# Two loads exchanged at the start, and two weight splits moved behind a bias and a sum, in a conditioned low-rank linear kernel

## The chip, the cores and the metric

The kernel runs on one core of one Trainium2 chip. The metric is device time in microseconds; the kernel before took 918.89 us, the median of three runs (918.77 to 919.0).

## The reference

For each of 128 batch entries (64 channels by 1024 columns) the input is first mixed over channels with one of 16 weight blocks of 64 by 64, chosen by an integer condition. The result y goes through a linear layer W with bias b (1024 to 1024) and, beside it, through eight low-rank maps of rank 16. The low-rank part m is scaled by a clamped ratio of norms, and x is added back:

```
y = einsum('bct,bcd->bdt', x, weights[condition])
z = einsum('bsd,od->bso', y, W) + b
u = einsum('bsd,edr->ebsr', y, A)
m = einsum('ebsr,ero,e->bso', u, B, p_scores)
gamma = minimum(0.5 * norm(z) / (norm(m) + 1e-6), 1.0)
out = x + z + gamma * m
```

All inputs and the output are float32.

## The kernel before

Two batch entries make a tile of 128 rows; there are 64 tiles in 32 pairs. The two tiles of a pair are called 0 and 1 (slots r = 0 and 1).

**Numbers in two parts.** TensorE multiplies in the type fp32r. Each operand is split in a high part, a cast on ACT (ScalarE), and a low part, the difference, on VectorE. A product is then three passes per chunk of 128 rows: high by high, high by low, low by high.

**Products of a pair.** W is cut in four quadrants W11, W12, W21, W22. Pair 0 uses them directly (`plain...`). From pair 1 on a scheme with seven products instead of eight runs, P1 to P7, on sums of y (S1 to S4) and of quadrants (T1 to T4): `product_y` and `product_s` at L984. P1 is y of tile 0 by W11, P2 by W21, P4 is y of tile 1 by T4, P6 is S2 by T2, P5 is S1 by T1, P7 is S3 by T3, P3 is S4 by W22. `down` and `up` are the low-rank part (L1049, L1053, L1068), and `mix` (L970) multiplies the next tiles by their mixer blocks.

**PSUM.** The bank b_ps is used by P1, P2, P6 and P7 in turn. P1's result leaves it in `bias_p1` (L796), and only then may P2 start. P2's leaves in `make_z11` (L775), after which P6 may start. m_ps is emptied by the sum of m1 (`add_m1`, L757), and then tile 0's `up` may start. The next pair's mix of tile 1 may overwrite a half of mix_ps once `split_y` (L691) has made the low part of the tile 0 that lay there.

**What sets the order.** Each engine has one written list of instructions and takes them in that order; semaphores join the lists. Nothing is planned at run time. SP and ACT also issue loads, each on a DMA queue of its own (q1 for SP, q10 for ACT in the profile).

**The start.** SP issues the load of the conditions, then x's tile 1, then waits for the conditions, issues the mixer blocks of half 0 of both tiles (`first_mixer`) and after them the chunks of W12 and W11 in turn (L286), W21, W22 and the rest. ACT issues x's tile 0 and, once the conditions are there, its mixer block for tile 0 (L533), W11's first chunk (L534) and its mixer block for tile 1 (L535). Then its computing starts with `split_w(W11, (0,))` (L438), followed by the copies of tile 0's y (L454) and of W12's first chunk. TensorE runs idle matmuls (L1090), mixes tile 0, makes two passes of W11's first chunk (L1003, L1005), mixes tile 1 (from x's tile 1 and the mixer blocks of tile 1), and goes on with `plain_first_half`.

**The stretch of pair 1.** The T matrices are made and split once, between 23 and 59 us. VectorE's order for pair 1 is: the low parts of T4 (two halves, L682), the low part of y's tile 1 and the sums S3 and S2 (L691, L699, L707), T2's first half, P1's bias, tile 1's residual of pair 0 (L852), gamma, m1's sum, T2's second half, S2's low part and so on. ACT casts the high parts of T4 and T2 ahead of the squares of z1 and m1 (L507, L516), with y's tile 1 between T2's halves.

Of the kernel before, what the change touches and what calls it, by code (L numbers as in the profile page):

```python
# [5 lines left out]
def conditioned_clamped_low_rank_linear_kernel(  # L6
# [29 lines left out]
    B, C, D = x.shape  # L36
    E = cond_w.shape[1]
    _, X, R = a.shape
    P = 128
    PER = P // C  # L40
# [9 lines left out]
    W11, W21, W22, T1, T2, T3, T4 = range(7)  # L50
# [7 lines left out]
    x_tiles = x.rearrange("(n q) c t -> n (q c) t", q=PER)  # L58
    out_tiles = out.rearrange("(n q) c t -> n (q c) t", q=PER)

    w_blocks = {n: w[h * H:(h + 1) * H, o * H:(o + 1) * H].rearrange("(k p) o -> k p o", p=P)
                for n, h, o in ((W11, 0, 0), (W12, 0, 1), (W21, 1, 0), (W22, 1, 1))}

    ctx = ExitStack()
    with ctx:  # L65
        def sb(name, shape, dt):
            return ctx.enter_context(nc.sbuf_tensor(name, shape, dt))
# [4 lines left out]
        def sem(name):  # L72
            return ctx.enter_context(nc.semaphore(name))
# [18 lines left out]
        x_in = sb("x_in", [P, 4, D], fp32)  # L92
# [22 lines left out]
        def stat(n, r):  # L115
            return stats[:, 6 + 2 * n + r:7 + 2 * n + r]
# [8 lines left out]
        raw11 = w_hi_raw[:, T1, :, :]  # L125
# [17 lines left out]
        x_loaded = [sem(f"x_loaded{s}") for s in range(4)]  # L143
# [3 lines left out]
        w_loaded = {n: [sem(f"w{name}_{k}_loaded") for k in range(HC)]  # L147
                    for n, name in ((W11, "11"), (W12, "12"), (W21, "21"), (W22, "22"))}
# [93 lines left out]
        def t_count(n, g):  # L242
            return 2 * T_ORDER.index(n) + g + 1


        def chunks(operand, g):
            return operand[:, 2 * g:2 * g + 2, :]
# [10 lines left out]
        def first_condition(engine, t, q):  # L258
            n = t * PER + q
            return engine.value_load(cond_ids[0:1, n:n + 1], min_val=0, max_val=E - 1)  # L260

        def first_mixer(t, q):
            return mixer[q * C:(q + 1) * C, t, q * C:(q + 1) * C]

        def cond_block(e):
            return cond_w[:, bass.ds(e, 1), :].rearrange("c e d -> c (e d)")

        def s_raw(n):
            return {S1: s14[:, 0, :, :], S4: s14[:, 1, :, :], S2: s23[:, 0, :, :], S3: s23[:, 1, :, :]}[n]
# [4 lines left out]
        def _(sp):  # L274
# [11 lines left out]
                    sp.dma_start(raw[n][:, k, :], w_blocks[n][k]).then_inc(w_loaded[n][k], 16)  # L286

            sp.dma_start(cond_ids[:, :], condition.rearrange("(o n) -> o n", o=1)).then_inc(ids_loaded, 16)
            sp.dma_start(x_in[:, 1, :], x_tiles[1]).then_inc(x_loaded[1], 16)
            sp.wait_ge(mixer_zeroed, 1)  # L290
            sp.wait_ge(ids_loaded, 16)
            sp.dma_start(first_mixer(0, 0), cond_block(first_condition(sp, 0, 0))).then_inc(mixer_loaded[0], 16)
# [140 lines left out]
        def _(act):  # L433
# [6 lines left out]
            def split_t(n, g):  # L440

                act.wait_ge({T1: t1_made, T2: t2_made, T3: t3_made, T4: t4_made}[n], g + 1)
                if n == T4:
                    act.wait_ge(plain_done, 4)
                elif n == T1:
                    act.wait_ge(t3_made, g + 1)
                elif n == T3:
                    act.wait_ge(t_lo_ready, t_count(T4, g))
                nc.scalar.copy(chunks(w_hi[:, n, :, :], g), chunks(raw_t[n], g)).then_inc(t_hi_ready, 1)

            def split_y(t, r, h, source=mixed):

                act.wait_ge(mix_done, halves(t, h))
                nc.scalar.copy(y_part(y_hi, r, h), source(h)).then_inc(y_hi_ready, 1)  # L454
# [7 lines left out]
            def split_s(p, n, first=False):  # L462

                act.wait_ge({S1: s1_made, S2: s2_made, S3: s3_made, S4: s4_made}[n], p)
                if not first:
                    act.wait_ge(p_done[{S1: 5, S2: 6, S3: 7, S4: 3}[n]], p - 1)
                nc.scalar.copy(s_hi[:, n, :, :], s_raw(n)).then_inc(s_hi_ready, 1)  # L467
# [30 lines left out]
            def square_z1(p, opening):  # L498

                act.wait_ge(z21_ready, p + 1)  # L500
                act.wait_ge(z22_ready, p + 1)
                if opening:
                    act.wait_ge(z12_squared, 1)
                else:
                    act.wait_ge(m_squared[0], p)
                    act.wait_ge(norm_z_ready[1], p)
                nc.scalar.activation(squares[:, :], z1[:, :], ACT.Square,  # L507
                                     accum_out=stat(Z_SQ, 1)).then_inc(z1_squared, 1)

            def square_m1(p, opening):  # L510

                act.wait_ge(m_done[1], p + 1)
                act.wait_ge(z1_squared, p + 1)
                if not opening:
                    act.wait_ge(norm_m_ready[1], p)
                nc.scalar.activation(squares[:, :], m_ps[:, :], ACT.Square,  # L516
                                     accum_out=stat(M_SQ, 1)).then_inc(m_squared[1], 1)
# [13 lines left out]
            act.wait_ge(mixer_zeroed, 1)  # L531
            act.wait_ge(ids_loaded, 16)
            act.dma_start(first_mixer(0, 1), cond_block(first_condition(act, 0, 1))).then_inc(mixer_loaded[0], 16)  # L533
            act.dma_start(raw11[:, 0, :], w_blocks[W11][0]).then_inc(w_loaded[W11][0], 16)  # L534
            act.dma_start(first_mixer(1, 1), cond_block(first_condition(act, 1, 1))).then_inc(mixer_loaded[1], 16)  # L535
            split_w(W11, (0,))
            split_y(0, 0, 0)
# [27 lines left out]
            split_t(T2, 0)  # L565
            for h in range(2):
                split_y(3, 1, h)
            split_t(T2, 1)
            square_z1(0, True)
            square_m1(0, True)  # L570
            split_s(1, S2, True)
            split_t(T1, 0)
            split_t(T1, 1)
            split_s(1, S3, True)
# [64 lines left out]
        def _(dve):  # L639
# [34 lines left out]
            def split_t(n, g):  # L674

                dve.wait_ge(t_hi_ready, t_count(n, g))
                if n == T2:
                    dve.wait_ge(t4_made, g + 1)
                    dve.wait_ge(t3_made, g + 1)
                elif n == T1:  # L680
                    dve.wait_ge(t2_made, g + 1)
                nc.vector.tensor_tensor(chunks(w_lo[:, n, :, :], g), chunks(raw_t[n], g),  # L682
                                        chunks(w_hi[:, n, :, :], g).bitcast(fp32), ALU.subtract
                                        ).then_inc(t_lo_ready, 1)

            def split_y(p, r, h, opening=False, source=mixed):

                dve.wait_ge(y_hi_ready, halves(2 * p + r, h))
                if r == 0 and not opening:
                    dve.wait_ge(y_copied, 2 * p + h - 1)  # L690
                nc.vector.tensor_tensor(y_part(y_lo, r, h), source(h), y_part(y_hi, r, h).bitcast(fp32),  # L691
                                        ALU.subtract).then_inc(y_lo_ready, 1)
# [33 lines left out]
            def make_half_over_m(p, r):  # L726

                dve.wait_ge(norm_m_ready[r], p + 1)
                nc.vector.tensor_scalar(stat(TWICE_M, r), stat(NORM_M, r), EPS, 1.0 / CLAMP, ALU.add,  # L729
                                        ALU.mult).then_inc(twice_m_ready[r], 1)  # L730
                dve.wait_ge(twice_m_ready[r], p + 1)
                nc.vector.reciprocal(stat(HALF_OVER_M, r), stat(TWICE_M, r)).then_inc(over_m_ready[r], 1)  # L732

            def limit_gamma(p, r):

                dve.wait_ge(norm_z_ready[r], p + 1)
                dve.wait_ge(over_m_ready[r], p + 1)  # L737
                nc.vector.tensor_scalar(stat(GAMMA, r), stat(NORM_Z, r), stat(HALF_OVER_M, r), 1.0, ALU.mult,  # L738
                                        ALU.min).then_inc(gamma_ready[r], 1)

            def make_gamma(p, r):

                make_half_over_m(p, r)
                limit_gamma(p, r)
# [8 lines left out]
            def add_m1(p):  # L753

                dve.wait_ge(gamma_ready[1], p + 1)
                dve.wait_ge(residual1_ready, p + 1)
                nc.vector.scalar_tensor_tensor(out=z1[:, :], in0=m_ps[:, :], scalar=stat(GAMMA, 1), in1=z1[:, :],  # L757
                                               op0=ALU.mult, op1=ALU.add).then_inc(out1_ready, 1)
# [34 lines left out]
            def bias_p1(p, par):  # L793

                dve.wait_ge(p_done[1], p)
                nc.vector.tensor_tensor(z0[:, par, up_], b_ps[:, :], bias[:, 1, :], ALU.add).then_inc(p1_biased, 1)  # L796
# [44 lines left out]
            dve.wait_ge(z12_squared, 1)  # L841
            nc.vector.tensor_tensor(z0[:, 0, :], z0[:, 0, :], x_in[:, 0, :], ALU.add).then_inc(residual0_ready, 2)
            split_t(T4, 0)
            split_t(T4, 1)
            split_y(1, 1, 0)
            make_s3(1, True)
            split_y(1, 1, 1)
            make_s2(1, True)
            split_t(T2, 0)
            bias_p1(1, 1)  # L850
            dve.wait_ge(z1_squared, 1)
            nc.vector.tensor_tensor(z1[:, :], z1[:, :], x_in[:, 1, :], ALU.add).then_inc(residual1_ready, 1)  # L852
            make_gamma(0, 1)
            add_m1(0)
            split_t(T2, 1)
            split_s(1, S2)
            dve.wait_ge(s2_made, 1)
# [375 lines left out]
```

## Time and profile before

| | us |
|---|---|
| median of three runs | 918.89 |
| profiled execution | 919.13 |
| its span | 917.3 |
| TensorE matmul busy | 908.7 (99%) |
| VectorE busy | 589.2 (64%) |
| ACT busy | 368.5 (40%) |
| GpSimd busy | 319.9 (35%) |

The busy times are shares of one profiled execution. The granted clock of TensorE is given as a share of full speed; over the whole span it was 0.999. TensorE's share says that the steady part is bound by its matmuls; the two places that the change touches lie in the first 63 us, where ACT and VectorE have more to do than later.

### The profile page before, as it was taken

How to read it: one execution, taken by the hardware profiler on the slowest of the kernel's cores; microseconds unless marked ns; L12 is line 12 of the kernel's file. 1: busy time of each engine (PE TensorE's matmuls, PEld its weight loads, DVE VectorE, ACT ScalarE, POOL GpSimd, SP SyncE). 2: the span in 40 equal slices, each digit the busy share in tenths (PEclk: the TensorE clock that was granted, in tenths of full speed). 3: DMA queues.
4: the chain of work that ended last, by engine and by line, in shares of the span. 5: the costliest groups of instructions: out<-in, count | busy, mean ns of one | idle time of the engine just before them, and what ended most of it. 6: DMA issues, size and time to landing. Idle time of an engine off the chain costs nothing. (4 is left out here: it accounts for less than half of the span.)

```text
span 917.3 us, 14774 instructions
## 1 busy us (share of the span) xinstructions
PE 908.7 (99%) x4642; PEld 773.7 (84%) x4642; DVE 589.2 (64%) x938; ACT 368.5 (40%) x732; POOL 319.9 (35%) x316
## 2 busy tenths in 40 slices
PE   8999999999999999999999999999999999999997
PEld 6888888888888888888888888888888888888886
DVE  6996757566665557665566656666655756566665
ACT  6653433434334334434343343334333443434333
POOL 0123443224433234432344332443323443224432
PEclk9999999999999999999999999999999999999999
DMA  8212222122221222211222212222112222122211
GB/s 295 81 71 95 95 72 83 37 91 94 71 94 46 71 94 81 85 68 49 94 94 71 94 40 78 94 71 94 49 68 94 94 71 79 40 93 94 73 47 69
DMA packets 32745, 75.17 MB, mean 82 GB/s; under 512 B 12761, under 2 KB 13786, under 8 KB 32730
## 3 DMA queue, kind: packets, MB, share of 16 engines
q1 hardware_dynamic: 32138, 73.91, 22.9%
q10 hardware_dynamic: 592, 1.08, 0.4%
q8 instruction: 7, 0.11, 0.1%
q14 instruction: 8, 0.07, 0.0%
HBM read 41.42 MB, written 33.55 MB: 82 GB/s over the span
## 5 line engine op out<-in xcount | busy, mean ns | idle before, releaser
L454 ACT CAST y<-mix_ps 128x512 fp32r<-128x512 f32 x126 | 74.3, 591 | 298.2 <-PE mix_ps L970 298.2
L386 POOL TENSOR_TENSOR stats<-stats 128x1 f32<-128x1 f32 x31 | 17.2, 556 | 451.2 <-ACT squares L507 451.2
L984 PE MATMUL b_ps<-w_hi,y 128*128 128x512 f32 x510 | 167.8, 389 | 0.0
L712 DVE TENSOR_TENSOR s_lo<-s,s_hi 128x512 fp32r<-128x512 f32 x124 | 134.6, 1105 | 4.2
L970 PEld LDWEIGHTS mix_ps<-mixer,x_in 128*128 128x128 f32 x1008 | 122.0, 191 | 6.8 <-issue 2.0
L970 PE MATMUL mix_ps<-mixer,x_in 128*128 128x128 f32 x1008 | 122.7, 275 | 1.2 <-DMA mixer<-in_L_cond_weights_dram 1.2
L467 ACT CAST s_hi<-s 128x512 fp32r<-128x512 f32 x124 | 76.7, 618 | 114.5 <-POOL s L360 93.4
L372 POOL TENSOR_TENSOR z<-z,x_in 128x512 f32<-128x512 f32 x61 | 79.1, 1296 | 113.8 <-ACT squares L488 107.3
L984 PEld LDWEIGHTS b_ps<-w_hi,y 128*128 128x128 f32 x510 | 95.7, 188 | 20.2 <-DVE z L796 0.3
L691 DVE TENSOR_TENSOR y<-mix_ps,y 128x512 fp32r<-128x512 f32 x126 | 86.4, 687 | 38.2 <-ACT s L460 38.2
L984 PE MATMUL b_ps<-w_lo,y 128*128 128x512 f32 x255 | 99.2, 389 | 0.0
L984 PE MATMUL c_ps<-w_hi,s_hi 128*128 128x512 f32 (+1 forms) x248 | 98.7, 398 | 0.0
L984 PE MATMUL c_ps<-w_lo,s_hi 128*128 128x512 f32 (+1 forms) x248 | 96.2, 388 | 0.0
L984 PE MATMUL c_ps<-w_hi,s_lo 128*128 128x512 f32 (+1 forms) x248 | 96.2, 388 | 0.0
L984 PE MATMUL b_ps<-w_lo,s_hi 128*128 128x512 f32 x244 | 94.9, 389 | 0.0
L984 PE MATMUL b_ps<-w_hi,s_hi 128*128 128x512 f32 x244 | 94.9, 389 | 0.0
L984 PE MATMUL b_ps<-w_hi,s_lo 128*128 128x512 f32 x244 | 94.9, 389 | 0.0
L984 PE MATMUL a_ps<-w_hi,y 128*128 128x512 f32 x264 | 87.1, 389 | 0.0
L770 DVE TENSOR_TENSOR z<-b_ps,z 128x512 f32<-128x512 f32 x30 | 20.8, 692 | 101.5 <-PE b_ps L984 101.5
L366 POOL TENSOR_TENSOR z<-z,x_in 128x1024 f32<-128x1024 f32 x30 | 72.1, 2404 | 0.0
L1049 PE MATMUL u_ps<-y,a_hi 128*128 128x512 f32 x256 | 69.3, 392 | 0.0
L791 DVE TENSOR_TENSOR z<-a_ps,bias 128x512 f32<-128x512 f32 x31 | 21.4, 691 | 57.7 <-PE a_ps L984 57.7
(156 smaller groups left out, 1584.9 us busy)
## 6 DMA issues: line engine op xcount, KB each, us to landing
x_in<-in_x_dram SPq DMA_DIRECT2D x63, 512.0 KB, 3.6
out_dram<-z SPq DMA_DIRECT2D x62, 512.0 KB, 2.8
w_lo_raw<-in_L_ffn_W_dram SPq DMA_DIRECT2D x8, 256.0 KB, 6.6
mixer<-in_L_cond_weights_dram SPq DMA_DIRECT2D x126, 16.0 KB, 2.1
w_hi_raw<-in_L_ffn_W_dram SPq DMA_DIRECT2D x7, 256.0 KB, 6.7
out_dram<-z SPq DMA_DIRECT2D x3, 256.0 KB, 2.0
x_in<-in_x_dram ACTq DMA_DIRECT2D x1, 512.0 KB, 3.3
a_lo_raw<-in_L_ffn_A_dram SPq DMA_DIRECT2D x1, 512.0 KB, 8.2
```

The lines of the kernel that those rows point to most:

```text
L366: nc.gpsimd.tensor_tensor(z1[:, :], z1[:, :], x_in[:, slot, :], ALU.add).then_inc(residual1_ready, 1)
L372: nc.gpsimd.tensor_tensor(z0[:, par, cols], z0[:, par, cols], x_in[:, 2 * par, cols], ALU.add).then_inc(residual0_ready, 1)
L386: nc.gpsimd.tensor_tensor(stat(NORM_Z, 1), stat(Z_SQ, 1), half, ALU.pow).then_inc(norm_z_ready[1], 1)
L454: nc.scalar.copy(y_part(y_hi, r, h), source(h)).then_inc(y_hi_ready, 1)
L467: nc.scalar.copy(s_hi[:, n, :, :], s_raw(n)).then_inc(s_hi_ready, 1)
L691: nc.vector.tensor_tensor(y_part(y_lo, r, h), source(h), y_part(y_hi, r, h).bitcast(fp32), ALU.subtract).then_inc(y_lo_ready, 1)
L712: nc.vector.tensor_tensor(s_lo[:, n, :, :], s_raw(n), s_hi[:, n, :, :].bitcast(fp32), ALU.subtract).then_inc(s_lo_ready, 1)
L770: nc.vector.tensor_tensor(z1[:, up_], bank[:, :], z0[:, par, up_], ALU.add).then_inc(u3_ready, 1)
L791: nc.vector.tensor_tensor(z1[:, lo], a_ps[:, :], bias[:, 2, :], ALU.add).then_inc(p4_biased, 1)
L970: made = nc.tensor.matmul(source(h)[:, k, :], x_in[:, slot, (h * HC + k) * P:(h * HC + k + 1) * P], mixer[:, r, :], start=True, stop=True)
L984: summed = nc.tensor.matmul(bank, left[:, k, :], right[:, n, k, c], start=(start and k == 0 and i == 0), stop=(stop and k == HC - 1 and i ...
L1049: return nc.tensor.matmul(u_ps[:, :], a_hi[:, k, :], y[:, k, :, :], start=(k == 0), stop=(k == KC - 1))
```

## The change

SP now issues W11's first chunk where it issued x's tile 1, and ACT issues x's tile 1 where it issued W11's first chunk. On ACT, T2's second half is cast after the squares of z1 and m1 and S2's high part. On VectorE the low parts of T4's second half and of T2's first half move: T4's behind P1's bias and tile 1's residual, T2's behind m1's sum. The number of instructions and of bytes is unchanged.

```diff
             sp.dma_start(cond_ids[:, :], condition.rearrange("(o n) -> o n", o=1)).then_inc(ids_loaded, 16)
-            sp.dma_start(x_in[:, 1, :], x_tiles[1]).then_inc(x_loaded[1], 16)
+            load_w(W11, (0,))
             sp.wait_ge(mixer_zeroed, 1)
             sp.wait_ge(ids_loaded, 16)
@@ on ACT
             act.dma_start(first_mixer(0, 1), cond_block(first_condition(act, 0, 1))).then_inc(mixer_loaded[0], 16)
-            act.dma_start(raw11[:, 0, :], w_blocks[W11][0]).then_inc(w_loaded[W11][0], 16)
+            act.dma_start(x_in[:, 1, :], x_tiles[1]).then_inc(x_loaded[1], 16)
             act.dma_start(first_mixer(1, 1), cond_block(first_condition(act, 1, 1))).then_inc(mixer_loaded[1], 16)
...
             for h in range(2):
                 split_y(3, 1, h)
-            split_t(T2, 1)
             square_z1(0, True)
             square_m1(0, True)
             split_s(1, S2, True)
+            split_t(T2, 1)
@@ on VectorE
             split_t(T4, 0)
-            split_t(T4, 1)
             split_y(1, 1, 0)
             make_s3(1, True)
             split_y(1, 1, 1)
             make_s2(1, True)
-            split_t(T2, 0)
             bias_p1(1, 1)
             dve.wait_ge(z1_squared, 1)
             nc.vector.tensor_tensor(z1[:, :], z1[:, :], x_in[:, 1, :], ALU.add).then_inc(residual1_ready, 1)
+            split_t(T4, 1)
             make_gamma(0, 1)
             add_m1(0)
+            split_t(T2, 0)
             split_t(T2, 1)
```

## Rows read from the trace of the kernel before

**Rows 1.** Busy, 11-62 us: PE, PEld, DVE, ACT, POOL, granted clock, DMA share, GB/s.
```profile
11.00:62.00 51.00, 51.00 (x256) 42.70 (x255) 49.98 (x70) 33.49 (x55) 5.46 (x5) 1.00 0.40 142
```

**Rows 2.** Order of time at the start: start us, us, instruction, idle before it.
```profile
3.99 0.59 ACTq L534 DMA_DIRECT2D w_hi_raw<-in_L_ffn_W_dram  x1
...
5.32 0.48 ACTq L535 DMA_DIRECT2D mixer<-in_L_cond_weights_dram  x1
...
5.84 2.02 PE L970 MATMUL mix_ps<-mixer,x_in 128*128 128x128 f32 x16 [1.25 <-DMA mixer<-in_L_cond_weights_dram]
...
7.00 0.62 ACT L438 CAST w_hi<-w_hi_raw 128x512 fp32r<-128x512 f32 x1 [4.34 <-DMA w_hi_raw<-in_L_ffn_W_dram]
...
8.73 1.95 PE L970 MATMUL m_ps<-mixer,x_in 128*128 128x128 f32 x16
8.95 0.62 ACT L438 CAST w_hi<-w_lo_raw 128x512 fp32r<-128x512 f32 x1 [0.36 <-DMA w_lo_raw<-in_L_ffn_W_dram]
...
10.43 0.69 DVE L691 TENSOR_TENSOR y<-m_ps,y 128x512 fp32r<-128x512 f32 x1
...
10.74 0.39 PE L984 MATMUL c_ps<-w_hi,y 128*128 128x512 f32 x1
...
11.43 0.39 PE L984 MATMUL a_ps<-w_hi,y 128*128 128x512 f32 x1
```

**Rows 3.** DMA issues at 1 to 2 and 5.2 to 5.8 us: KB, us to landing.
```profile
x_in<-in_x_dram SPq DMA_DIRECT2D x1, 512.0 KB, 4.2
...
mixer<-in_L_cond_weights_dram ACTq DMA_DIRECT2D x1, 16.0 KB, 3.2
```

**Rows 4.** The page's part 6, all mixer loads of SP: KB, median us to landing.
```profile
mixer<-in_L_cond_weights_dram SPq DMA_DIRECT2D x126, 16.0 KB, 2.1
```

**Rows 5.** Half microseconds from 6.0 on, columns as in rows 1.
```profile
6.00:6.50 0.50, 0.50 (x6) 0.50 (x6) 0.00 (x0) 0.00 (x0) 0.00 (x0) 1.00 0.40 129
6.50:7.00 0.50, 0.50 (x7) 0.50 (x6) 0.00 (x0) 0.00 (x1) 0.00 (x0) 1.00 0.38 99
7.00:7.50 0.50, 0.50 (x7) 0.50 (x6) 0.00 (x0) 0.50 (x1) 0.00 (x0) 1.00 0.86 305
```

**Rows 6.** Order of time on VectorE (DVE) from 35 to 69 us.
```profile
35.16 0.69 DVE L691 TENSOR_TENSOR y<-mix_ps,y 128x512 fp32r<-128x512 f32 x1 [0.29 <-ACT s L460]
...
38.63 2.35 DVE L682 TENSOR_TENSOR w_lo<-w_hi_raw,w_hi 128x1024 fp32r<-128x1024 f32 x2
...
42.70 0.68 DVE L707 TENSOR_TENSOR s<-mix_ps,s 128x512 f32<-128x512 f32 x1
...
44.43 0.68 DVE L796 TENSOR_TENSOR z<-b_ps,bias 128x512 f32<-128x512 f32 x1
...
46.86 1.28 DVE L757 SCALAR_TENSOR_TENSOR z<-m_ps,stats,z 128x1024 f32<-128x1024 f32 x1
...
51.53 0.69 DVE L775 TENSOR_TENSOR z<-b_ps,bias 128x512 f32<-128x512 f32 x1
...
61.71 1.28 DVE L691 TENSOR_TENSOR y<-mix_ps,y 128x512 fp32r<-128x512 f32 x2
...
68.73 0.69 DVE L780 TENSOR_TENSOR z<-c_ps,z 128x512 f32<-128x512 f32 x1 [1.23 <-PE c_ps L984]
```

**Rows 7.** Who waited for whom, 38 to 63 us: total us, times, longest.
```profile
PEld m_ps L1068 <- DVE z L757: 0.4, 1, 0.4
...
PEld b_ps L984 <- DVE z L796: 0.3, 1, 0.3
```

**Rows 8.** Order of time on TensorE (PE) from 42 to 63 us.
```profile
42.08 0.39 PE L984 MATMUL b_ps<-w_hi,y 128*128 128x512 f32 x1
...
52.46 0.39 PE L984 MATMUL b_ps<-w_hi,s_hi 128*128 128x512 f32 x1
...
62.21 0.39 PE L984 MATMUL b_ps<-w_hi,s_lo 128*128 128x512 f32 x1
...
62.54 0.68 PE L970 MATMUL mix_ps<-mixer,x_in 128*128 128x128 f32 x4
```

## The prediction, made before the changed kernel was run

> **What bounds the kernel now.** I read the busy times by stretch first. From 11 to 62 us TensorE is busy for all of it and VectorE for 49.98 us of 51.00 [rows 1]; the reader should see that two engines are full at once there, and that a TensorE on 100% says nothing of short waits, since ends of matmuls are modelled. So I went on to the order of time at the start, for the two loads that change places [rows 2], then to the times from issue to landing [rows 3, 4] and to the DMA's free share [rows 5], then to VectorE's order of time in the stretch where the splits move [rows 6], and last to TensorE's waits and starts there [rows 7, 8]. The spacing of 512-column matmuls is 0.23 us (three of them from 10.74 to 11.43 [rows 2]).
>
> Two things come out. The start is a chain: the mixer block lets the first mix begin at 5.84, ACT then holds tile 0's copy back because it casts W11's first chunk only at 7.00, and the mix of tile 1 starts at 8.73 [rows 2]. Later, from 35.16 on, VectorE has no wait ahead of an instruction until 68.73, where it idles 1.23 us for TensorE [rows 6]. In that run its y split at 61.71 ends at 62.39, and TensorE's next mix begins at 62.54 [rows 6, 8], where the product ahead would have let it go at 62.44 (its last matmul starts at 62.21, one spacing earlier). So at 62.54 TensorE is released by VectorE, by 0.10 us, and whatever TensorE won before that point is lost in that wait unless VectorE's own chain gets shorter. From there on VectorE has slack, so what the kernel's end moves by is what the start at 62.54 moves by.
>
> **The loads.** Let g be the time by which TensorE's work after the start moves ahead. W11's first chunk is now issued at SP's second place and lands well before the 7.00 at which ACT now starts on it [rows 2]. ACT (0.62 us) and VectorE split it while TensorE waits for the mixer block. That block's issue doesn't move, nor do I move the 5.84: bounds 0.2 us earlier (fewer bytes ahead) and 0.2 later; I take 0. ACT copies tile 0's first half as soon as the first half of the mix ends, near 6.95 and not at 7.52 (behind 7.00 and 0.62), so the two first passes of W11 follow the mix at 7.86 (5.84 and 2.02) and are over by about 8.1, where before they were followed at 8.73.
>
> Then comes tile 1's mix, which wants two things. x's tile 1 is issued at 3.99 on ACT's queue in place of a load half its size: x's tile 1 took 4.2 us to landing when it stood behind tile 0's load [rows 3], so it is there at 8.2 at the latest that I expect. ACT's mixer block for tile 1 is issued behind it at 5.32 and took 3.2, landing at 8.5 [rows 2, 3]; at the median of 2.1 [rows 4] it would be there at 7.4. So the mix starts at 8.6 if nothing changes for that block (g is 0.1), at 8.2 if it comes early. The next term is W12's first chunk: ACT starts on it at 8.95, having waited for the DMA [rows 2]. Between 6.0 and 7.0 the DMA engines were at 0.40 and 0.38 of their time [rows 5], 0.61 us free in all. The half us after it moved 305 GB/s at a share of 0.86 [rows 5], 355 at full share, by which the added 256 KB want 0.74 us of all engines. So I count W12 as 0.1 us late; the bounds are 0 and the whole 0.7. VectorE's parts of that chunk and of y, 0.60 each, then end near 10.9 and not at 11.11 (10.43 and 0.68), which lets the product on y of tile 1 start up to 0.3 before its 11.43 [rows 2]. g is therefore at most 0.3, and at least -0.4 (0.7 of lateness less the 0.3). I take 0.2, between the 0.1 of an unchanged mixer block and the 0.3.
>
> The Trainium skill's DMA: Bandwidth & Descriptors, section Queues, rings and completion order, says that each DMA engine goes round-robin over the queues that have work and serves one packet of descriptors of one queue before it takes the next. In the trace the mixer block issued at 5.32 took 3.2 us against a median of 2.1 [rows 3, 4], as if on some engines W12 of the other queue had gone ahead of it. By the rule that block would now stand right behind x's tile 1 and before W12, g would be 0.3, and the sum 0.1 us lower: that is rival (e).
>
> **Does g reach 62.54?** VectorE's run begins at 35.16 with a wait of 0.29 us for ACT's copy of the mix [rows 6], which TensorE releases; no other wait stands in it. So VectorE's chain moves by g with TensorE, both ways.
>
> **The moved splits.** On VectorE a 1024-column split takes 1.13 us of the engine and a 512-column operation 0.60: 38.63 to 42.70 is two and three of them, 42.70 to 44.43 one and one [rows 6]. Before, p1's bias starts at 44.43. Now T4's second part and T2's first part are no longer ahead of it, and the queue reaches it at 38.63 + 1.13 + 4 x 0.60 = 42.16. But it waits for P1, whose last matmul starts at 42.08 and ends 0.39 later [rows 8]; with 0.03 for the release, an estimate, VectorE starts at 42.50. So 0.34 us of idle time goes into a run that had none. It hits the work behind it: residual of tile 1 (1.13), T4's part (1.13), gamma (0.70: 44.43 + 0.60 + 1.13 is 46.16, and m1's sum starts at 46.86 [rows 6]) and m1's sum, which now starts at 46.06 and not at 46.86, then both parts of T2. From there on the set of finished work is that of before, 0.34 later: z11 at 51.87 instead of 51.53, the y split of 61.71 at 62.05.
>
> On TensorE two waits go: for p1's bias (the loader idle 0.3) and for m1's sum (0.4) [rows 7]. Less the 0.04 between loads that is usual, that is at most 0.6 us; by starts of matmuls I make it 0.46. It comes at P6, which started at 52.46 [rows 8], by then about 0.55 earlier, and finds z11 unready: 51.87 and 0.69 are 52.56, and so it starts at 52.62. The stall removed is late again as a stall on z11. Even without it TensorE would stand at the mix of 62.54 until y's split, now 0.34 later. On ACT, T2's second cast stands behind the squares of z1 and m1 now; TensorE wants T2 at P6, 8 us later, and the squares come sooner for it. The transfers that residual 1 and m1's sum release start 0.8 to 2 us earlier, in a stretch where the DMA has room (share 0.40 over the 51 us [rows 1]). I count these at 0; bounds 0.1 either way.
>
> **Sum.** Start -0.2 (+0.4 to -0.3), VectorE's new wait +0.34 (0 to 0.35), the removed TensorE waits 0 (down to -0.10, the wait at 62.54 that would go if VectorE were earlier). That is +0.14. The profiled execution took 919.13 (span 917.3), so 919.27 for one like it; the median of the three runs, 918.89, is 0.24 below it, which makes 919.03.
>
> **Rivals.** What a measurement here can tell from no change is about 0.2%, 1.84 us.
> (a) *The reordering pays.* TensorE's removed waits stay won because VectorE isn't what releases it at 62.54 and P1's end is met without idle time: -0.46 - 0.2, 918.2. For it: the waits of rows 7 are real. Against: a run of 26 us without a wait on VectorE. Half of it, no idle time of 0.34 but the wait at 62.54 kept, gives 918.7.
> (b) *The loads are late.* Tile 1's 512 KB and the mixer block behind it collide with W12's first chunk on the DMA engines; it decides from the point where that chunk lands over 0.25 us after the 8.95 of before. ACT casts it ahead of y, so TensorE stands at the product on y. At 0.7 late g is -0.4, and with the 0.34 that is 919.6. For it: ACT already waits for that load. Against: the free 0.6 us between 6.0 and 7.0 [rows 5].
> (c) *The clock falls.* If TensorE stands longer before tile 1's mix and the granted clock goes to the lower of its levels (1.2 instead of 2.4 GHz), the 4 us of matmuls from 8.73 take twice as long: 923. Against: the granted clock is 1.00, and the wait before 5.84, over a microsecond long, did not lower it.
> (d) *Nothing moves*: VectorE finds P1 done, the start is bound by W12 alone, g is 0 to 0.1, and nothing is added: 918.8 to 918.9.
> (e) *The mixer block gains.* Tile 1's block lands about 1 us earlier, at its median of 2.1 from issue, since W12 is no longer served ahead of parts of it; then g is its full 0.3 and the time 919.13 - 0.3 + 0.34 - 0.24 = 918.93. For it: the 3.2 us of rows 3 with the DMA at 0.4 of its time. Against: it still stands behind a load, now of twice the bytes. It is what the Trainium skill's rule on queues gives.
>
> **How the numbers follow.** Forecast, the wait on P1 taking back the start's gain (918.9 to 919.3): 0.25; (d) 0.1; (e) 0.17, the same wait on P1 with the larger g. (a) in whole or half: 0.2. (b): 0.25. (c) 0.03. For the range I take from half of (a) up through (b), with 0.1 us of scatter of a median: 918.4 to 919.7. By the bound of 0.2% only (c) and something unforeseen leave "same": same 0.94, slower 0.04, faster 0.02.
>
> **What would show it.** In the changed kernel's order of time: ACT's cast of W11 before 5.84 and its y cast at about 7.0; the mix of tile 1 between 8.2 and 8.7; on VectorE a wait of 0.3 us on b_ps ahead of p1's bias near 42.3; no wait on VectorE at the TensorE starts of P2 and of up(0), but one on z11 at P6; the mix of 62.54 at 62.68, still right behind the y split. Wrong would be: W12's cast after 9.2, no idle time before p1's bias, or a mix near 62.5 that comes straight behind the product.

## The result, and the profile after

The changed kernel took 920.16 us (median of 22 runs, 919.75 to 921.53) against 918.87 (22 runs, 918.62 to 920.83): a ratio of 1.0015, 95% interval 1.001 to 1.0021. It is 1.29 us slower, where 919.03 was forecast and 919.7 was the upper end. The profiled execution took 920.47 with a span of 918.6 and a granted clock of 0.999.

The start of the changed kernel in order of time (start us, us, instruction, idle before it); these lines answer to [rows 2]:

```profile
3.55 0.59 ACTq L534 DMA_DIRECT2D x_in<-in_x_dram  x1
...
4.87 0.48 ACTq L535 DMA_DIRECT2D mixer<-in_L_cond_weights_dram  x1
...
5.40 0.62 ACT L438 CAST w_hi<-w_hi_raw 128x512 fp32r<-128x512 f32 x1 [2.75 <-DMA w_hi_raw<-in_L_ffn_W_dram]
5.80 2.16 PE L970 MATMUL mix_ps<-mixer,x_in 128*128 128x128 f32 x16 [0.38 <-DMA mixer<-in_L_cond_weights_dram]
...
8.07 0.40 PE L1005 MATMUL b_ps<-w_lo,y 128*128 128x512 f32 x1
...
9.21 2.02 PE L970 MATMUL m_ps<-mixer,x_in 128*128 128x128 f32 x16 [0.74 <-DMA mixer<-in_L_cond_weights_dram]
9.56 0.62 ACT L438 CAST w_hi<-w_lo_raw 128x512 fp32r<-128x512 f32 x1 [0.98 <-DMA w_lo_raw<-in_L_ffn_W_dram]
...
11.31 0.40 PE L984 MATMUL c_ps<-w_hi,y 128*128 128x512 f32 x1
```

W11's cast is early and the passes on it end before 8.5, as meant. In this execution what they won is spent in a wait for tile 1's mixer block, and tile 1's mix starts at 9.21 instead of 8.73. The repeat of the changed kernel (e1 below) was as slow by another way: its mixes are early, and TensorE waits for the low part of W12's first chunk, which ACT casts at 9.59. Its lines:

```profile
8.46 2.02 PE L970 MATMUL m_ps<-mixer,x_in 128*128 128x128 f32 x16 [0.65 <-DMA mixer<-in_L_cond_weights_dram]
...
9.59 0.62 ACT L438 CAST w_hi<-w_lo_raw 128x512 fp32r<-128x512 f32 x1 [1.67 <-DMA w_lo_raw<-in_L_ffn_W_dram]
...
11.08 0.47 PE L984 MATMUL c_ps<-w_hi,y 128*128 128x512 f32 x1 [0.36 <-DVE w_lo L644]
```

So two loads are late, and which of them TensorE feels differs from one execution to the next; W12's cast is late in both. The DMA issues of the changed kernel from 4.8 to 5 us, and those from 3 to 4.2 (KB, us to landing), say when the block and x's tile 1 were there; they answer to [rows 3]:

```profile
mixer<-in_L_cond_weights_dram ACTq DMA_DIRECT2D x1, 16.0 KB, 4.2
...
x_in<-in_x_dram ACTq DMA_DIRECT2D x1, 512.0 KB, 3.6
```

x's tile 1 was there at 7.15, two microseconds before it was used. The block behind it took 4.2 us instead of 3.2; in the repeat it took 3.4, where the kernel before took 3.4 in its own repeat (e13), so the 4.2 is no fixed cost. In the half microseconds from 6.5 on (columns as in [rows 1], to be read against [rows 5]), the DMA engines moved little in this execution:

```profile
6.50:7.00 0.50, 0.50 (x7) 0.50 (x6) 0.24 (x1) 0.00 (x0) 0.00 (x0) 1.00 0.44 91
7.00:7.50 0.50, 0.50 (x7) 0.50 (x6) 0.00 (x0) 0.40 (x1) 0.00 (x0) 1.00 0.41 37
7.50:8.00 0.50, 0.50 (x6) 0.50 (x5) 0.28 (x1) 0.19 (x2) 0.00 (x0) 1.00 0.14 31
```

In the repeat the share in these slices is 0.50, 0.65 and 0.90, and W12's first chunk landed 4.7 us behind its issue in both. The low share is therefore not the mark of the loss.

VectorE in the changed kernel, which answers to [rows 6]:

```profile
42.14 0.68 DVE L707 TENSOR_TENSOR s<-mix_ps,s 128x512 f32<-128x512 f32 x1
43.08 0.69 DVE L796 TENSOR_TENSOR z<-b_ps,bias 128x512 f32<-128x512 f32 x1 [0.27 <-PE b_ps L984]
...
46.14 0.16 DVE L732 RECIPROCAL stats<-stats 128x1 f32<-128x1 f32 x1
46.85 0.21 DVE L738 TENSOR_SCALAR stats<-stats 128x1 f32<-128x1 f32 x1 [0.54 <-DVE stats L732]
47.10 1.28 DVE L757 SCALAR_TENSOR_TENSOR z<-m_ps,stats,z 128x1024 f32<-128x1024 f32 x1
...
63.08 1.28 DVE L691 TENSOR_TENSOR y<-mix_ps,y 128x512 fp32r<-128x512 f32 x2
```

Two waits stand in the run that had none. From S2's making to P1's bias it is 0.94 us and not 0.60: the forecast 0.34. The second wasn't forecast: 0.54 us idle ahead of gamma's last step (L738), though nothing that it waits for is late. Before the change the same step came 0.27 us after the start of the reciprocal ahead of it, now 0.71, so it adds 0.43 or 0.44. The two lines before the change:

```profile
46.34 0.16 DVE L732 RECIPROCAL stats<-stats 128x1 f32<-128x1 f32 x1
46.61 0.21 DVE L738 TENSOR_SCALAR stats<-stats 128x1 f32<-128x1 f32 x1
```

On TensorE, to be read against [rows 8]:

```profile
53.73 0.47 PE L984 MATMUL b_ps<-w_hi,s_hi 128*128 128x512 f32 x1 [0.88 <-DVE z L775]
...
63.91 1.35 PE L970 MATMUL mix_ps<-mixer,x_in 128*128 128x128 f32 x10
```

P6 stands 0.88 us for z11, and the mix of 62.54 comes at 63.91, right behind the y split that ends at 63.76. TensorE's wait for P1's bias is gone; the one for m1's sum, which was forecast to go, is still 0.3 us instead of 0.4, since m1's sum stands behind gamma. Nothing of what was won is left at 63.91.

### The profile page after: what moved, and what is told of

The parts are those of the page before. It is cut to its first block and busy times, and to the rows that moved or that the text cites. A ratio compares the mean times of both kernels' runs of the same rounds, so it can differ in the third digit from the quotient of the medians.

```text
span 918.6 us, 14774 instructions
## 1 busy us (share of the span) xinstructions
PE 909.6 (99%) x4642; PEld 773.8 (84%) x4642; DVE 589.3 (64%) x938; ACT 368.3 (40%) x732; POOL 319.0 (35%) x316
```

## The experiments

Two starts of mixes divide the time of every run. A is the mix of tile 0 of pair 1 (31.91 before), up to which only the loads matter. B is the mix of 62.54. What follows B is the profiled time less B; it is nearly constant (856.55 to 856.66) in all but e5, e10 and e11. The first column is the median less that of the kernel before on the same chip (22 runs of the changed kernel, 8 of e8, 11 of every other; 15 to 33 of before). The other columns are from one profiled execution each.

| run | median, less before | A | B | B - A | profiled time - B |
|---|---|---|---|---|---|
| before | | 31.91 | 62.54 | 30.63 | 856.59 |
| e13 before again | -0.08 | 31.83 | 62.46 | 30.63 | 856.57 |
| changed | +1.29 | 32.49 | 63.91 | 31.42 | 856.56 |
| e1 changed again | +1.31 | 32.37 | 63.83 | 31.45 | 856.56 |
| e2 loads only | +0.55 | 31.87 | 62.51 | 30.63 | 856.66 |
| e14 loads again | +0.54 | 32.14 | 62.78 | 30.63 | 856.59 |
| e3 splits only | +0.77 | 31.69 | 63.14 | 31.45 | 856.58 |
| e4 T4 before the bias | +0.46 | 31.47 | 62.52 | 31.06 | 856.55 |
| e5 waits added | +0.57 | 31.69 | 62.68 | 30.99 | 856.76 |
| e6 T2 before gamma | +0.33 | 31.95 | 62.94 | 30.99 | 856.56 |
| e7 block first | +0.91 | 32.83 | 63.47 | 30.63 | 856.56 |
| e8 both early | +2.50 | 32.89 | 63.52 | 30.63 | 856.56 |
| e9 x in halves | +0.31 | 31.77 | 62.39 | 30.62 | 856.56 |
| e10 residual on GpSimd | +0.61 | 32.29 | 63.35 | 31.06 | 856.72 |
| e11 e4 with waits | +0.38 | 32.15 | 62.77 | 30.63 | 856.78 |
| e12 half of x | +0.29 | 31.55 | 62.17 | 30.63 | 856.62 |
| e15 half of x again | +0.03 | 32.04 | 62.67 | 30.63 | 856.58 |

How to read it: B - A takes three values over 30.63, and each returns to within 0.03 wherever its cause is there. A scatters by 0.8 us (31.47 to 32.29) over the eight profiles with the loads of before, so a single profile says little of the start, and medians are used for it. An estimate of A in the median run is the median less the last two columns: 31.6 to 31.7 with the loads of before (but 31.8 in e11), 32.1 to 32.2 with the exchange. What decides A lies in the first 11 us: from the first product on c_ps (10.74 before, 11.31 in the changed kernel) to A it is 21.17 to 21.29 us in all 17 profiles. The runs' ratios have 95% intervals of 0.0009 either way (0.8 us), which includes most of these differences; it is B - A, together with the medians of 11, that carries the verdicts.

**The change again, and its two parts.** e1 is the changed kernel, e2 the first two hunks of the diff alone (SP's and ACT's loads), e3 all the others alone.

> The changed kernel once more, as a control. Its profile had tile 1's mix at 9.22 us (8.73 before), the first product on c_ps at 11.31 (10.74), 0.27 us of idle time ahead of P1's bias and 0.54 us ahead of gamma's last step, and the mix of 62.54 at 63.91. Theory: all of these come from the order of instructions and repeat, so about 1.3 us over before. Rival: the late start and the wait in gamma are scatter of one execution; then the mix of pair 1 comes at 62.9 to 63.9 in different runs and the median gain over before is smaller than in the profile.

> Only the exchange of W11's first chunk and x's tile 1; splits as before. Theory (the start's loss reaches the end): tile 1's mix near 9.2, c_ps near 11.3, the mix of 62.54 at 63.1, and 0.58 us over before (919.45 where before is 918.87). Rival (the prediction's g): the exchange gains 0.2 us when alone, 918.7. Rival 2: VectorE's slack takes the loss in and the time is that of before.

> Only the moved splits on ACT and VectorE; loads as before. Theory: 0.34 us idle ahead of P1's bias and 0.44 more than usual ahead of gamma's last step, TensorE stands on z11 at P6, the mix of 62.54 at 63.3; 0.78 us over before (919.65). Rival: the wait in gamma hangs on the moment at which loads or other engines work, and is not there: only 0.34 over before (919.2).

Ratios 1.0013 (1.0004 to 1.0022), 1.0007 (0.9998 to 1.0016), 1.0008 (0.9999 to 1.0018). The parts add up: 0.55 and 0.77 are 1.32, against 1.31. The loads act on A alone, the splits on B - A alone, by 0.82, with the wait in gamma in it. VectorE's slack takes in nothing. Not all that was expected repeated: tile 1's mix starts at 8.46 in e1 and at 8.60 in e2, and not near 9.2, and e2's B is 62.51 and not 63.1. The profile of e2 is of a fast execution (919.17, median 919.39), and its 0.55 rests on the median; e14 repeats it with 0.54.

**P1's wait alone taken away.** e4 is e3 with one line moved:

```diff
             make_s2(1, True)
+            split_t(T4, 1)
             bias_p1(1, 1)
...
-            split_t(T4, 1)
             make_gamma(0, 1)
```

> As the run with only the splits moved, but T4's second part stands behind S2 and ahead of P1's bias, where VectorE waited for P1. Theory: no idle time ahead of the bias, so 0.34 less than the run with only the splits moved; with the wait in gamma kept (its place in VectorE's list is the same) 0.44 over before (919.3). Rival: that wait hangs on time and goes too; then VectorE's chain is that of before, and the time is that of before or 0.1 less (918.8).

Measured: +0.46, ratio 1.0006 (0.9997 to 1.0015); B - A falls by 0.39 to 31.06, and no idle time is left ahead of the bias. The wait in gamma stayed, as the profile of e4 shows, and is the whole of what is left (0.43):

```profile
45.47 0.21 DVE L738 TENSOR_SCALAR stats<-stats 128x1 f32<-128x1 f32 x1 [0.54 <-DVE stats L732]
```

**What the wait in gamma hangs on.** e5 is e3 with waits that are fulfilled long before; e6 is e3 with T2's first part moved; e11 has the edits of e4 and e5.

```diff
             split_t(T4, 0)
+            dve.wait_ge(idle_set, 1)
+            dve.wait_ge(mixer_zeroed, 1)
+            dve.wait_ge(w_hi_ready, 1)
+            dve.wait_ge(a_hi_ready, 1)
             split_y(1, 1, 0)
```

```diff
             split_t(T4, 1)
+            split_t(T2, 0)
             make_gamma(0, 1)
             add_m1(0)
-            split_t(T2, 0)
             split_t(T2, 1)
```

> As the run with only the splits moved (its profile: 0.54 us idle ahead of gamma's last step, 0.11 before the change), with four waits that are long fulfilled put into VectorE's list behind T4's first part, where VectorE is busy: gamma's instructions stand two places further down VectorE's list, as before the change, and nothing else moves. Theory (the 0.43 hangs on the place of an instruction in VectorE's list, as code loading would): 0.11 again, and 0.34 over before (919.2) instead of 0.78. Rival (it hangs on what stands ahead of gamma, T4's second part, or on what other engines do at that time): 0.54 stays, and the time with it.

> As the run with only the splits moved, but T2's first part ahead of gamma and m1's sum instead of behind them. Theory (place in the list): gamma's last step stands where it stood before the change, so the 0.43 goes and only the 0.34 us of idle time ahead of P1's bias stay: 919.2. TensorE then waits for m1's sum at 48.2 and not only for z11. Rival (what matters is T4's part before gamma or the changed order of the squares on ACT): 0.54 stays idle, 919.6.

> The run with T4's second part ahead of P1's bias and the four fulfilled waits put behind T4's first part. Theory: neither the idle time ahead of P1's bias nor the 0.43 in gamma is there, VectorE's chain is as long as before the change, and so the mix comes 30.6 us after that of tile 0 of pair 1, as before; at the end the two places further down cost the 0.2 us that the run with the waits had in its last step. 919.05; without these 0.2, 918.85. Rival: the reordering costs by something else that these two waits only accompany; 919.3.

e5, then e6, in the order of time on VectorE:

```profile
45.34 0.16 DVE L732 RECIPROCAL stats<-stats 128x1 f32<-128x1 f32 x1
45.61 0.21 DVE L738 TENSOR_SCALAR stats<-stats 128x1 f32<-128x1 f32 x1
```

```profile
46.75 0.17 DVE L732 RECIPROCAL stats<-stats 128x1 f32<-128x1 f32 x1
47.02 0.21 DVE L738 TENSOR_SCALAR stats<-stats 128x1 f32<-128x1 f32 x1
```

In both the wait is gone, and B - A is 30.99, that is 0.36 for P1's wait alone. e5 changes no work and keeps T4's part ahead of gamma, so neither that nor what other engines do at the time makes the wait: the place in the list does. The packed traces say which place. They hold a record of each instruction of VectorE, waits that stand by themselves among them; the four waits of e5 come out as two records more than in e3. Gamma's last step is the 64th record of VectorE in all five profiles with 0.54 us ahead of it (changed, e1, e3, e4, e10), and the 66th in the twelve with 0.11. A second such place is the 192nd record. In the kernel before it is gamma's last step of a later pair; in e11, where that step is the 194th, the wait is gone, and in e10 (described below), where it is the 190th, the wait stands ahead of the sum behind it, which is now the 192nd. Before, e11, e10:

```profile
110.71 0.21 DVE L738 TENSOR_SCALAR stats<-stats 128x1 f32<-128x1 f32 x1 [0.47 <-DVE stats L732]
```

```profile
110.58 0.21 DVE L738 TENSOR_SCALAR stats<-stats 128x1 f32<-128x1 f32 x1
```

```profile
111.86 1.28 DVE L752 SCALAR_TENSOR_TENSOR z<-m_ps,stats,z 128x1024 f32<-128x1024 f32 x1 [0.49 <-DVE stats L740]
```

In e11 both waits of the changed kernel are gone and B - A is that of before. e5 and e11 cost more than their B - A says (+0.57 and +0.38); 0.2 of it is behind B, and the chain of waits at the end shows where. e5's, and behind it that of the kernel before (start us, us, what):

```profile
913.47 0.23 issue
913.69 0.75 DVE z L966
```

```profile
913.36 0.03 issue
913.38 0.75 DVE z L962
```

The same two places further down that take the wait out of gamma of pair 0 put one of 0.23 instead of 0.03 ahead of the last sum. The remaining 0.2 of e11 lies in A (32.15 in its profile), though its loads are those of before; that is open. e11's time is therefore 0.2 over the 919.05 that was expected, and it is B - A that says that the two waits are all that the moved splits cost.

**Less work on VectorE.** e10 is the kernel before, with its first residual on GpSimd:

```diff
@@ VectorE
-            dve.wait_ge(z11_squared, 1)
-            dve.wait_ge(z12_squared, 1)
-            nc.vector.tensor_tensor(z0[:, 0, :], z0[:, 0, :], x_in[:, 0, :], ALU.add).then_inc(residual0_ready, 2)
@@ GpSimd
+                        residual0(0, 0, 0)
+                        residual0(0, 0, 1)
                         norm_z1(0)
```

> The kernel before with one edit: the residual of pair 0's tile 0 (1.13 us of VectorE at 37.5) is done by GpSimd in two halves. Theory (VectorE's chain sets the mix of 62.54): the chain is 1.13 us shorter, TensorE's waits at 45.2, 48.2 and 62.5 all go, and the mix follows its product at once: 0.56 us less, 918.3. By the theory of the place in the list gamma's instructions now stand two places up, as in the changed kernel, and its last step is preceded by 0.54 us idle although no split was moved; the shorter chain hides it. Rival: GpSimd's adds slow VectorE down by as much, or the chain is bound elsewhere; 918.9.

Measured: +0.61, ratio 1.0007 (0.9998 to 1.0016), the opposite sign; the rival had it, but for the wait in gamma, which isn't hidden. In order of time, e10 around its residual:

```profile
36.12 1.28 POOL L372 TENSOR_TENSOR z<-z,x_in 128x512 f32<-128x512 f32 x1 [6.21 <-ACT squares L497]
36.15 2.34 DVE L673 TENSOR_TENSOR w_hi_raw<-w_hi_raw,w_lo_raw 128x1024 f32<-128x1024 f32 x1
...
47.42 0.21 DVE L740 TENSOR_SCALAR stats<-stats 128x1 f32<-128x1 f32 x1 [0.54 <-DVE stats L734]
```

The subtraction that makes T4's second half (L673) took 2.34 us instead of 1.22 beside GpSimd's add of 1.28: the 1.13 us taken off VectorE came back in the same place. So e10 does not show what a shorter chain on VectorE would give. Then comes the wait in gamma, of 0.54 as forecast, in a kernel in which no split was moved; two records were taken out ahead of it. B - A is 31.06, as in e4, the other run with that wait alone. e10 has 0.14 more behind B; that was not followed up.

**The loads.** e7 is e2 with ACT's last two issues exchanged; e8 is e2 with x's tile 1 on SP:

```diff
@@ e7, ACT
-            act.dma_start(x_in[:, 1, :], x_tiles[1]).then_inc(x_loaded[1], 16)
             act.dma_start(first_mixer(1, 1), cond_block(first_condition(act, 1, 1))).then_inc(mixer_loaded[1], 16)
+            act.dma_start(x_in[:, 1, :], x_tiles[1]).then_inc(x_loaded[1], 16)
@@ e8, SP (and ACT's load of x's tile 1 taken out)
             load_w(W11, (0,))
+            sp.dma_start(x_in[:, 1, :], x_tiles[1]).then_inc(x_loaded[1], 16)
```

> The exchanged loads alone, but ACT issues tile 1's mixer block ahead of x's tile 1. Theory 1 (the loss comes from the block standing behind 512 KB): the block lands by 7.2, tile 1's mix starts as soon as x's tile 1 is there, near 8.0, and the loss of 0.55 us of the exchange goes: 918.8 to 918.9. Theory 2 (W12's first chunk sets it, landing at 8.9 to 9.6 behind x's tile 1, against 8.6 to 8.9 before): tile 1's mix is early but the product on c_ps stays near 11, and the time is 919.2 to 919.5.

> The loads alone, but x's tile 1 on SP's queue right behind W11's first chunk, both ahead of the mixer blocks; ACT issues only x's tile 0 and its two blocks. Theory 1 and 2 both: nothing stands between the blocks and W12, which land by 7.5 and 8.7; the first mix is 0.3 to 0.6 us late, as the blocks of tile 0 stand behind 256 KB more, the mix of tile 1 starts at about 8.5. 918.8. If the bytes ahead of the blocks cost their whole 0.6 us, 919.2.

e7: +0.91, ratio 1.0008 (0.9999 to 1.0017); e8: 1.0027 (1.0017 to 1.0038). Both theories of e7 were too kind: the block was early, but x's tile 1 landed so late that TensorE waited for it, and W12's first chunk was cast at 10.09. e7's order of time:

```profile
9.05 2.05 PE L970 MATMUL m_ps<-mixer,x_in 128*128 128x128 f32 x16 [0.62 <-DMA x_in<-in_x_dram]
10.09 0.62 ACT L438 CAST w_hi<-w_lo_raw 128x512 fp32r<-128x512 f32 x1 [1.55 <-DMA w_lo_raw<-in_L_ffn_W_dram]
```

In e8 the first mix starts 1.5 us later than before, not 0.3 to 0.6, and the time is 2.2 us over the upper one of its two expectations; this profile is of one of its faster executions (920.08, median 921.39):

```profile
7.32 2.02 PE L970 MATMUL mix_ps<-mixer,x_in 128*128 128x128 f32 x16 [1.90 <-DMA mixer<-in_L_cond_weights_dram]
```

e9 puts half of x's tile 1 back to the early place; e12 and e15 load only half of it at all:

```diff
@@ e9, from the kernel before
-            sp.dma_start(x_in[:, 1, :], x_tiles[1]).then_inc(x_loaded[1], 16)
+            load_w(W11, (0,))
+            sp.dma_start(x_in[:, 1, lo], x_tiles[1][:, lo]).then_inc(x_loaded[1], 16)
...
-            act.dma_start(raw11[:, 0, :], w_blocks[W11][0]).then_inc(w_loaded[W11][0], 16)
+            act.dma_start(x_in[:, 1, up_], x_tiles[1][:, up_]).then_inc(x1_up_loaded, 16)
@@ e12 and e15, from e2
-            act.dma_start(x_in[:, 1, :], x_tiles[1]).then_inc(x_loaded[1], 16)
+            act.dma_start(x_in[:, 1, lo], x_tiles[1][:, lo]).then_inc(x_loaded[1], 16)
...
+            nc.gpsimd.memset(x_in[:, 1, up_], 0.0).then_inc(upper_set, 1)
```

> Splits as before. W11's first chunk and x's tile 1's lower half (256 KB) at SP's early place, the upper half (256 KB, rows of 2 KB) where the changed kernel has the whole tile on ACT: the bytes at each place are those of the kernel before, W11's early cast stays. Theory (the exchange loses since 256 KB more go out on ACT's queue between the mixer blocks, in front of tile 1's block and of W12): the loss of 0.55 us goes, W12's first chunk is cast at 8.6 to 9.0, and the time is 918.6 to 918.9. Rival (it is W11 that must be last there, or the order of the queues as such): W12 is cast at 9.2 to 9.6 and the time stays at 919.3 or above.

> The exchanged loads alone, splits as before; but ACT loads only the lower half of x's tile 1 (256 KB instead of 512), and GpSimd sets the upper half to zero early, so that half's values are left out for this one tile. Order, queues and number of DMA issues are those of the exchange. Theory (the bytes in front of tile 1's mixer block and of W12 are what the exchange costs): tile 1's block and x are there by 8.2, W12's first chunk is cast by 8.9, the mix of tile 0 of pair 1 comes at 31.3 to 31.7 and the time is 918.6 to 918.9. Rival (the exchange costs by its order, whatever the size): W12 is cast at 9.2 or later and the loss of 0.3 us or more stays.

> The kernel before once more, for a second profile of its start. Its first profile had tile 1's mix at 8.73, W12's cast at 8.95 and pair 1's first mix at 31.91; that execution was 0.24 us over the median. Theory: a usual execution has pair 1's first mix near 31.7, as the runs with the loads of before had (31.47 to 31.95).

> The exchanged loads alone, again. Theory (512 KB in front of tile 1's block and W12): W12's cast at 9.0 to 9.6, pair 1's first mix at 31.9 to 32.5, 0.5 us over before. Rival: the first run's 0.55 us was scatter, and it is within 0.2 us of before.

> The exchanged loads with half of x's tile 1 left out, again. If its 0.29 us over before was scatter, as its profile (pair 1's first mix at 31.55) says, it is now within 0.15 us of before; if the order of the loads costs something whatever their size, 0.3 us over before again, half of what the whole exchange costs.

Ratios: e9 1.0005 (0.9996 to 1.0014), e12 1.0004 (0.9995 to 1.0013), e13 1.0 (0.9991 to 1.001), e14 1.0005 (0.9996 to 1.0014), e15 1.0001 (0.9992 to 1.001). e13, e14 and e15 came out by their theories. e9 and e12 did so in their profiles, but their medians (+0.31 and +0.29) are over what was expected. With 256 KB in that place W12's first chunk is cast at 8.74 in e9's profile, 8.59 in e12's and 9.09 in e15's, where the issues stand 0.4 us later. From its issue it took 3.7 to 3.8 us in these three, 3.5 to 4.1 in the eight with the loads of before, and 4.1 to 4.7 in the four with the whole exchange. The time that TensorE waited for tile 1's block, from who waited for whom between 8 and 9.5 us, in the changed kernel, e14 and e15:

```profile
PE m_ps L970 <- DMA mixer<-in_L_cond_weights_dram: 0.7, 1, 0.7
```

```profile
PE m_ps L970 <- DMA mixer<-in_L_cond_weights_dram: 0.4, 1, 0.4
```

```profile
PE m_ps L972 <- DMA mixer<-in_L_cond_weights_dram: 0.2, 1, 0.2
```

Over their 22 runs, the exchange with all of x (e2, e14) has a median of 919.46 and with half of it (e12, e15) of 919.00. So about 0.45 of the 0.55 us go with the bytes (runs of several chips are taken together here). The 0.13 that stay over 918.87 are within what two runs of one kernel differ by (e12 and e15: 0.14), and e9's 0.31 is not explained by bytes: it is open whether the order costs something of its own. No run tells the share of the late block from that of the late W12.

## Why the prediction was wrong

- **What bounds it** was right. The time after B is constant within 0.11 us in all but e5, e10 and e11, and what is put into VectorE's chain (0.36, 0.43 or both) comes out at B in full.
- **The start failed.** g was put at +0.2 (from -0.4 to +0.3); it was -0.55 by the medians. The step that failed is the one on the DMA: "0.61 us free in all", from which W12 was counted 0.1 us late, and with it tile 1's mix "at 8.6 if nothing changes for that block". The forecast priced the added 256 KB at 0.74 us of all engines and let the free time take in most of it. W12's first chunk in fact took 4.5 us from issue to landing (median of the four profiles with the whole exchange) against 3.7 (median of the eight with the loads of before): about the whole 0.74. The block took 3.4 to 4.2 us against 2.8 to 3.6, and TensorE waited for it in all four (0.2 to 0.7 us) and in none of the eight, which spent what W11's early cast had won. A free share was read as room. In the four profiles the share from 6.5 to 7.5 is again below 1 (0.18 to 0.77), so the added bytes did not fill the pause; why the engines pause there isn't shown. The bound of -0.4 was from W12 alone; the block had no later end at all, only "unchanged" and "early".
- **The rule on queues** (rival (e)) went the other way. By the Trainium skill's DMA: Bandwidth & Descriptors, section Queues, rings and completion order, the prediction had the block right behind x's tile 1 and 1 us earlier than before. In the four profiles it landed 1.0 to 1.9 us behind x's tile 1, and from its issue it took 3.4 to 4.2 us, never the 2.1 of the rival. That section says only that each DMA engine takes turns between the queues, packet by packet; that the block would land earlier was the prediction's own inference.
- **g reaches 62.54**: right, by e2 and e14 (B - A 30.63), with a negative g.
- **P1's wait**: right in place and size: 0.34 forecast, 0.36 in e5 and e6, and moved away with e4.
- **The removed waits of TensorE**: right, worth nothing: they came back as the wait on z11 at P6 (0.88 us), and the y split bounds B.
- **The sum lacked a term.** Gamma was taken as 0.70 us, the duration of the old place. It took 1.14, by the place of its last step in VectorE's list. The sum by what was measured is 0.55 + 0.34 + 0.43 = 1.32, against 1.29; the forecast sum was 0.14, and of what it missed 0.75 is the start's and 0.43 gamma's.
- Rival (b) had the sign, the place and the W12 chunk (cast at 9.56), and decided from the point it named, 0.25 us after 8.95; its 919.6 lacks gamma's 0.43 and the block. That it came near is in part luck: it had no term for gamma, and its start was 0.15 short. (a) and (d) are refuted; (c) did not come about: the granted clock was 1.00 in the half microseconds with the wait for the block (8.5 to 9.5) too.
- **Two numbers of the working** don't follow from what stands beside them: 10.9 instead of 11.11 gives 0.2 for the product on y of tile 1 and not 0.3, and half of (a) less 0.1 of scatter is 918.6 and not the 918.4 of the range. Neither would have changed the outcome.

## What to carry to other kernels

Do not count a DMA share below 1 in a short stretch after an issue as room, as here the load beside the added 256 KB landed 0.8 us later, the whole time of those bytes: ask which small load queued behind the moved bytes is waited for, and give its landing a later end as well. When an engine's list is moved in a stretch where it has no slack, a new wait on a product that used to be done in time costs in full, and the other engine's removed waits are worth nothing until that chain is shorter. An instruction of VectorE that moves by two places can gain or lose 0.43 us by the place alone, so compare its idle time with a run in which only places change. Differences of half a microsecond are best cut at fixed events into stretches, of which some repeat far better than the whole time (here A to B, within 0.03 us).

## What was not expected of the hardware

- A fixed instruction of VectorE waits 0.43 us or not by its place in the list: 0.54 us idle in the changed kernel, e1, e3, e4 and e10, 0.11 in before, e2, e5 to e9 and e11 to e15, and never another value. Four fulfilled waits (e5) take it away, two records less (e10) bring it. The places found are VectorE's 64th and 192nd record, and one near the kernel's end (0.2 us, in e5 and e11). Code loading would do that, but no run shows it. The Trainium skill's Runtime: NRT & Kernel Launch, section Instruction fetch mechanics, says that an engine's instruction memory is refilled in blocks while it works on, mostly hidden; if that is what is seen here, 0.43 us of it aren't hidden among instructions as short as 0.15 to 0.2 us. The section gives blocks of 256 instructions, and the two places lie 128 records apart, so its figure does not fit as it stands.
- GpSimd's add of 128x512 (1.28 us) stretched a VectorE subtraction of 128x1024 that ran at the same time from 1.22 to 2.34 us (e10, one profile).
- e8's runs lie in two groups, two near 920.05 and five from 921.3 to 921.6, with one at 922.7. Its profile, at 920.08, is of the first group; where the second group loses its 1.3 us isn't shown.
